# A decoder layer on one core: masks and context requested earlier, the convolution by four groups, and filters without the D_skip products

## Time and profile before

| | us |
|---|---|
| median of 3 runs | 7834.85 (7827.19 to 7838.27) |
| profiled execution, time | 7831.92 |
| its span | 7830.1 |
| setup, to its end | 194.0 |
| pass 1 | 5297.0 |
| pass 2 | 202.0 |
| pass 3 | 2137.1 |

### The profile page before, as it was taken

One profiled execution on the slowest core, in us unless ns is written; L12 is line 12 of the kernel. 1 busy time (PEld: TensorE's weight loads), 2 busy tenths in 40 slices (PEclk: granted clock), 3 DMA queues, 4 the chain that ended last, 5 costly groups with the idle time before them and its releaser, 6 DMA issues. The chain is left out here.

```text
span 7830.1 us, 109010 instructions
## 1 busy us (share of the span) xinstructions
PE 6972.0 (89%) x25744; PEld 3853.7 (49%) x25744; DVE 5404.5 (69%) x13954; ACT 4454.2 (57%) x9788; POOL 4638.6 (59%) x3991
## 2 busy tenths in 40 slices
PE   4799999999999999999999999996569999999997
PEld 2344444444444444444444444443535655556554
DVE  4477888778887888778877788776235555555554
ACT  1677887778777877777877887774211111111111
POOL 0588888888888888888888888884011111111111
PEclk5899999999999999999999999997889999999998
DMA  0465555555565555655555555552720000000000
GB/s 18 108 148 139 141 133 139 152 136 137 130 149 143 141 134 136 152 138 138 131 149 143 141 134 136 154 135 69 239 75 33 33 30 30 30 30 30 30 30 19
DMA packets 489840, 843.53 MB, mean 108 GB/s; under 512 B 35612, under 2 KB 139174, under 8 KB 487594
## 3 DMA queue, kind: packets, MB, share of 16 engines
q1 hardware_dynamic: 472234, 820.42, 41.2%
q10 hardware_dynamic: 17024, 16.78, 0.6%
HBM read 754.24 MB, written 82.84 MB: 107 GB/s over the span
## 5 line engine op out<-in xcount | busy, mean ns | idle before, releaser
L1203 POOL TENSOR_TENSOR arena<-arena 128x512 f32<-128x512 f32 x2048 | 2593.3, 1282 | 286.9 <-DVE arena L1128 245.6
L825 PE MATMUL psum<-arena 128*128 128x512 f32 x4096 | 2216.5, 636 | 216.5 <-POOL arena L1203 209.4
L1128 DVE TENSOR_TENSOR_SCAN arena<-arena,psum 128x512 f32<-128x512 f32 x1024 | 1238.0, 1209 | 386.3 <-ACT arena L997 294.7
L1216 POOL TENSOR_TENSOR arena<-arena 128x512 f32<-128x512 f32 x1024 | 1347.5, 1316 | 113.4 <-PE psum L825 113.3
L984 ACT ACTIVATE arena<-arena 128x128 f32<-128x128 f32 x4096 | 1303.1, 395 | 129.9 <-PE psum L810 129.7
L1132 DVE TENSOR_TENSOR_SCAN arena<-psum,arena 128x512 f32<-128x512 f32 x1024 | 1237.5, 1208 | 107.1 <-ACT psum L997 41.4
L825 PEld LDWEIGHTS psum<-arena 128*128 128x128 f32 x4096 | 714.4, 201 | 775.0 <-POOL arena L1203 422.0
L1800 POOL TENSOR_SCALAR arena<-arena 128x4 f32<-128x4 f32 x160 | 36.8, 230 | 1262.4 <-DVE arena L1666 1262.3
L997 ACT ACTIVATE arena<-arena 128x508 f32<-128x508 f32 x1024 | 737.6, 720 | 58.4 <-DVE arena L1128 57.6
L810 PEld LDWEIGHTS psum<-arena 128*128 128x128 f32 x4096 | 525.4, 147 | 489.8 <-issue 446.6
L997 ACT ACTIVATE psum<-arena 128x508 f32<-128x508 f32 x1024 | 699.7, 683 | 65.2 <-DVE arena L1132 31.7
(11 more groups left out here) (216 smaller groups left out, 10588.2 us busy)
## 6 DMA issues: line engine op xcount, KB each, us to landing
arena<-bc_scratch SPq DMA_DIRECT2D x1152, 512.0 KB, 5.1
arena<-in_xT_dram SPq DMA_DIRECT2D x32, 512.0 KB
arena<-in_x_dram SPq DMA_DIRECT2D x32, 512.0 KB, 8.6
x_scratch<-arena SPq DMA_DIRECT2D x32, 512.0 KB, 5.8
xin_scratch<-arena SPq DMA_DIRECT2D x64, 256.0 KB, 3.1
arena<-kernel_scratch SPq DMA_DIRECT2D x32, 512.0 KB, 4.0
arena<-y_scratch SPq DMA_DIRECT2D x32, 512.0 KB
arena<-x_scratch SPq DMA_DIRECT2D x32, 512.0 KB, 3.7
```

What stands on the lines that cost most here:

```text
L825: pe.matmul(y_ps, ident, ring[:, u % RING], start=False, stop=n == NS - 1).then_inc(S["nsum"], 1)
L1128: dve.tensor_tensor_scan(s, decay_sb[:, u // 2 % 2], bx_ps[:, u // 2 % 2], 0.0, ALU.mult, ALU.add)\
L1203: pool.tensor_tensor(h, h, Cb[:, u // 2 % PAIRS, u % 2], ALU.mult).then_inc(S["hc"], 1)
L1216: pool.tensor_tensor(ring[:, u % RING], uu[par][:, c], Bb[:, state(u)], ALU.mult)\
```

## The change

- In pass 1 the masks and the transposed context are no longer requested at v = 2 of the block that uses them, but at v = 16 of the block before (`load_ahead`), once the block before that has used them. What stays in `load_back` is x and the context.
- `xin_scratch` and `y_scratch` have four groups of 64 channels. Pass 1 stores a block with four transfers in rows of 256 B instead of two in rows of 512 B; pass 3 loads y with four transfers in rows of 256 B instead of one in rows of 4 KB.
- Pass 2 runs by these groups. ACT issues all loads of x, and two of the first four tables; SP issues the other tables and all stores. A group is stored when its two rounds are read out. The loops are written out, and a bank of PSUM is waited for alone instead of with its whole round. Rows of x and y are now 16 KB in both directions.
- In setup the second product of each channel goes. `D_skip` is added by eight DVE operations of 8 x 32 elements after ACT's copies, from a tile whose last row it is loaded into.

```diff
             for q in range(8):
                 for dd in range(32):
-                    pe.matmul(o, tab[:, NR:NR + NG, d], tab[:, 0:NR, d], start=True, stop=False)
-                    mm = pe.matmul(o, last8, drow[:, d], start=False, stop=True)
+                    mm = pe.matmul(o, tab[:, NR:NR + NG, d], tab[:, 0:NR, d], start=True, stop=True)
                 mm.then_inc(kmm, 1)
...
+            for q in range(8):
+                dve.wait_ge(ksb, q + 1)
+                own = at_last[:, 32 * q:32 * q + 32]
+                dve.tensor_tensor(own, own, dsk[:, 32 * q:32 * q + 32], ALU.add).then_inc(skipped, 1)
...
-                need(sp, "k_mm", i - 1, 1)
+                need(sp, "xa_mm", i - 1, 2)
+                sp.dma_start(ctxn, i_["ctx"][:, bass.ts(i, G), :]).then_inc(S["ld_ctx"], 16)
+
+            def load_ahead(i):
+                need_apart(sp, ("maskb", i - 1, 1), ("tmb", i - 1, 1), ("k_mm", i - 1, 1))
+                sp.dma_start(tmask8, ...); sp.dma_start(mask8, ...)
                 sp.dma_start(ctxT0, ...); sp.dma_start(ctxT1, ...)
...
-                for h in range(DH):
-                    sp.dma_start(xin_d[h][:, bass.ts(i, G), :], xn[:, :, h * P:(h + 1) * P]).then_inc(S["st_xin"], 16)
+                for g in range(D // DG):
+                    sp.dma_start(xin_d[g][:, bass.ts(i, G), :], xn[:, :, g * DG:(g + 1) * DG])\
+                      .then_inc(S["st_xin"], 16)
...
+                    if v == 16:
+                        load_ahead(i)
...
+            load_toeplitz(sp, 0, 0)
+            load_toeplitz(sp, 0, 1)
+            for q in range(1, ROUNDS):
                 for k in range(NB_):
+                    sp.wait_ge(turned[k], q)
+                    load_toeplitz(sp, q, k)
+                if q > PER_GROUP and q % PER_GROUP == 1:
+                    store_y(q // PER_GROUP - 1)
+            store_y(D // DG - 1)
...
-                            pe.wait_ge(out_s if n % 2 else out_v, q * NB_)
+                            pe.wait_ge(out_s if n % 2 else out_v, (q - 1) * NB_ + n // 2 + 1)
...
+            load_toeplitz(act, 0, 2)
+            load_x(act, 0)
+            load_toeplitz(act, 0, 3)
+            for g in range(1, D // DG):
+                load_x(act, g)
...
-                    sp.dma_start(y, y_d[:, bass.ts(i, G), :]).then_inc(S["g_y"], 16)
+                    for g in range(D // DG):
+                        sp.dma_start(y[:, :, g * DG:(g + 1) * DG], y_d[g][:, bass.ts(i, G), :]).then_inc(S["g_y"], 16)
```

More of the change, by code:

```diff
@@ L29 @@
 DH = D // P
+DG = 64
 DI = 512
@@ L1246, in pass2 @@
     NB_ = 4
-    LOOPS = P // (GD * NB_)
+    ROUND = GD * NB_
+    ROUNDS = D // ROUND
+    PER_GROUP = DG // ROUND
     with ExitStack() as ctx:
@@ L1250, in sem @@
             return sems.named(n)
-        x_ld = [sem(f"x_ld{h}") for h in range(DH)]
+        x_ld = [sem(f"x_ld{g}") for g in range(D // DG)]
         t_ld = [sem(f"toeplitz_ld{k}") for k in range(NB_)]
@@ L1255, in pass2 @@
         cv = Carve(arena)
-        x2 = [cv.f32(B * P).rearrange("p (b d) -> p b d", b=B) for _ in range(DH)]
+        x2 = [cv.f32(B * DG).rearrange("p (b d) -> p b d", b=B) for _ in range(D // DG)]
         rev, tz = ([cv.f32(GD * L).rearrange("p (d j) -> p d j", d=GD) for _ in range(NB_)] for _ in range(2))
         block = ctx.enter_context(nc.Block())
[L1259 to L1270, removed]
+        def load_x(eng, g):
+            for q in range(2):
+                w = B // 2
+                eng.dma_start(x2[g][:, q * w:(q + 1) * w], xin_d[g][:, q * w:(q + 1) * w]).then_inc(x_ld[g], 16)
+        def load_toeplitz(eng, q, k):
+            row = kr_d[q * ROUND + k * GD:q * ROUND + (k + 1) * GD, :]
+            src = bass.AP(row.tensor, row.offset, [[1, P], [2 * L, GD], [1, L]])
+            eng.dma_start(rev[k], src).then_inc(t_ld[k], 16)
@@ L1272, in _, with channels @@
+        def channels(q, first, n):
+            d = q % PER_GROUP * ROUND + first
+            return x2[q // PER_GROUP][:, :, d:d + n]
         @block.sync
         def _(sp):
-            def load_toeplitz(q, first):
-                for k in range(NB_):
[L1277 to L1293, removed]
+            def store_y(g):
+                w = B // 2
+                for h in range(2):
+                    sp.wait_ge(out_v, NB_ * PER_GROUP * (g + 1))
+                    sp.wait_ge(out_s, NB_ * PER_GROUP * (g + 1))
+                    sp.dma_start(y_d[g][:, h * w:(h + 1) * w], x2[g][:, h * w:(h + 1) * w]).then_inc(y_st, 16)
@@ L1296, in _ @@
+            load_toeplitz(sp, 0, 0)
+            load_toeplitz(sp, 0, 1)
+            for q in range(1, ROUNDS):
+                for k in range(NB_):
+                    sp.wait_ge(turned[k], q)
[3 more added lines that the diff above has]
+            store_y(D // DG - 1)
+            sp.wait_ge(y_st, 16 * 2 * (D // DG))
         @block.tensor
         def _(pe):
-            def products(h, q, first):
+            for q in range(ROUNDS):
+                if q % PER_GROUP == 0:
+                    pe.wait_ge(x_ld[q // PER_GROUP], 16 * 2)
@@ L1302, in products @@
                         n = 2 * k + j
-                        if not first:
-                            pe.wait_ge(out_s if n % 2 else out_v, q * NB_)
+                        if q:
+                            pe.wait_ge(out_s if n % 2 else out_v, (q - 1) * NB_ + n // 2 + 1)
                         for dd in range(4):
-                            d = k * GD + j * 4 + dd
-                            col = x2[h][:, :, bass.ds(q * (NB_ * GD) + (d - h * P), 1)]
+                            col = channels(q, 4 * n + dd, 1)
                             pe.matmul(psum[:, n, dd * B:(dd + 1) * B], tz[k][:, j * 4 + dd],
@@ L1311, in products, with turn @@
                               .then_inc(conv_mm, 1)
[L1313 to L1328, removed]
-            copy(tz[k], rev[k][:, :, ::-1]).then_inc(turned[k], 1)
+        def turn(eng, copy, k, q):
+            eng.wait_ge(t_ld[k], 16 * (q + 1))
+            if q:
+                eng.wait_ge(conv_mm, (q - 1) * ROUND + (k + 1) * GD)
+            copy(tz[k], rev[k][:, :, ::-1]).then_inc(turned[k], 1)
@@ new lines, in read_out @@
+        def read_out(eng, odd, sem_, copy, turns):
+            for k in turns:
+                turn(eng, copy, k, 0)
+            for q in range(ROUNDS):
+                for n in range(odd, 2 * NB_, 2):
+                    eng.wait_ge(conv_mm, q * ROUND + 4 * (n + 1))
+                    copy(channels(q, 4 * n, 4).rearrange("p b d -> p d b"),
+                         psum[:, n, 0:4 * B].rearrange("p (d b) -> p d b", d=4)).then_inc(sem_, 1)
+                    if q + 1 < ROUNDS and n // 2 in turns:
+                        turn(eng, copy, n // 2, q + 1)
@@ L1331, in _ @@
         @block.gpsimd
         def _(pool):
[L1333 to L1340, removed]
-                    eng.wait_ge(conv_mm, q * (NB_ * GD) + 4 * (n + 1))
-                    dst = x2[h][:, :, bass.ds(q * (NB_ * GD) + (4 * n - h * P), 4)]
-                    copy(dst.rearrange("p b d -> p d b"),
-                         psum[:, n, 0:4 * B].rearrange("p (d b) -> p d b", d=4)).then_inc(sem_, 1)
-                    if ahead and n // 2 in turns:
-                        turn(eng, copy, n // 2, q + 1, False)
-            for k in turns:
-                turn(eng, copy, k, 0, True)
-            for h in range(DH):
-                last = h == DH - 1
-                with eng.Fori(h * LOOPS, (h + 1) * LOOPS - last, 1) as q:
-                    one_round(h, q, True)
-                if last:
-                    one_round(h, DH * LOOPS - 1, False)
+            for q in range(ROUNDS):
+                turn(pool, pool.tensor_copy, 0, q)
@@ L1362, in _ @@
         def _(act):
[L1363 to L1364 removed]
+            load_toeplitz(act, 0, 2)
[3 more added lines that the diff above has]
+                load_x(act, g)
             read_out(act, 1, out_s, act.copy, (2,))
[L1366 to L1369 removed]
 PER3 = dict(
[L1374 removed]
+    g_y=64, g_x1=16, g_xa=32, st_out=16,
     fo_mm=4, fo_mul=4, fo_add=4, xt=1, hn0=4, hn1=4, ht_mm=2, hT=2,
```

49 lines of the change are left out of this document (18 added, 31 removed).

## The result

The changed kernel takes 7473.8 us (median of 4 runs, 7461.07 to 7475.96) against 7831.02 (4 runs) before: a ratio of 0.954 [0.9523, 0.9556], or 357 us less. The prediction said 307 us less, 7525, with a range of 7455 to 7645. The profiled execution took 7475.96 us; its span is 7474.2.

| us | before | after | measured | predicted |
|---|---|---|---|---|
| setup | 194.0 | 133.6 | -60.4 | -39 |
| pass 1 | 5297.0 | 5039.9 | -257.1 | -237 + 1.8 |
| pass 2 | 202.0 | 163.1 | -38.9 | -35 |
| pass 3 | 2137.1 | 2137.6 | +0.5 | +2.3 |

A forecast was written before the change was run, and what follows sets the result against it. POOL's wait for the mask transfer, with PE stalled behind it, was taken to hold pass 1. From 7831.92 us: -237 (pass 1) -39 (setup) -35 (pass 2) +1.8 +2.3 = -307, so 7525 us, range 7455 to 7645.

The forecast's parts named there:

- What bounds the kernel: Pass 1: POOL's 237.2 us idle before the mask step, 7.41 us each, makes PE wait 6.1 us per block.
- The two signs at the block's start: Pass 1: the third chunk's taps start near 8 us after the first's; PE's granted clock is 1.00 at block start.
- I take the wait itself, 7.41 us: Pass 1: removing POOL's mask wait returns its 7.41 us in each of 32 blocks, 237 us.
- The control (block 0): Pass 1's block without a mask step: taps' spacing 7.94 us against 13.96, so 6.02 of 6.61 us come back.
- PE's whole account comes back: Rival, pass 1: PE regains 6.1 us standing and 3.3 low clock per block; 300 instead of 237, 7462 us; chance 0.15.
- The first rival: Pass 1: another wait steps in, POOL waiting for the scans; half the gain, 7644 us, period above 155; chance 0.15.
- v = 16 costs nothing: Pass 1: SP's four extra transfers and a wait at v = 16 hardly delay the next C load; cost nothing.
- 256-byte rows: zero in the blocks: Pass 1: the x store's 2048 packets take 3.6 us instead of 1.8, hidden by the second C load's slack; cost zero.
- the terms +1.8 and +2.3: Packet-count costs of 256-byte rows: +1.8 us for the last store ahead of pass 2, +2.3 at pass 3's start.
- both products take an equal part: Setup: each filter's two products share 78.4 us equally, so dropping one saves 39.2; gain 39 us, low end 20.
- its own steps: Pass 2: PE starts 14.7 us in, stands 18 us for starved round 1 tables, then a shorter store tail; gain 35.
- The rival without starving: Pass 2: round 1's tables aren't starved beside the x loads; gain 55 instead of 35 us, 7505 us; chance 0.08.

The follow-up runs named there:

- masks ahead: The kernel before with only the masks and the transposed context requested at v = 16: 7573.95 us, ratio 0.9679.
- the step later: The kernel before with POOL's mask step at unit 12 instead of unit 4, every transfer left in place: 7582.4 us, ratio 0.9691.
- masks alone ahead: The changed kernel with the transposed context requested at v = 2 again and only the two masks at v = 16: 7476.37 us, ratio 0.9553.
- the two reordered kernels: The changed kernel with x groups 1 to 3 requested at rounds 0, 2, 4: 7460.26 us; with all pass 2 transfers on SP's queue: 7465.75 us.
- the second stall removed in this kernel: The changed kernel with PE's scores of the third sequence at unit 38 instead of 36, removing the wait at L779: 7476.96 us, ratio 0.9553.
- the pairs over 128 rows: The kernel before with each filter's second product summed over 128 rows, zeros but for the first, instead of one: 7778.27 us in one run.
- 24 smaller ones: The changed kernel with each x group loaded by eight transfers in rows of 4 KB instead of two of 16 KB: 7471.64 us, ratio 0.9544.

## Why the prediction was right, and where a size was off

- **What bounds the kernel: right.** POOL's wait for the mask, with PE behind it, was the largest thing to remove. Three kernels show it: masks ahead (pass 1 5042.1), the step later (5047.0), masks alone ahead (5038.6), against 5297.0. The two signs at the block's start came as named: spacing of the taps 7.69 us (near 8), clock 1.00.
- **Size of pass 1: 257 instead of 237.** The step "I take the wait itself, 7.41 us" was some 0.6 us per block too small. It counted POOL's wait and nothing for the clock. Measured, PE gives back 175.9 / 32 = 5.5 us of standing and 81.2 / 32 = 2.5 us of slow clock, 8.0 together; the two parts of PE's account had been 6.1 and 3.3. The period fell by 8.1 us, to 151.9 and not 152.6. The 20 us are less than the 29 by which the same pass differs between kernels (5025.7 to 5054.9). The averages of four kernels with the old pass 1 and four with the new one, 5293.4 and 5039.5, differ by 254, so the term was too small, by about 17. The control (block 0) had been read for POOL's and DVE's work only, and is one block that itself starts at low clock. The rival "PE's whole account comes back" (300) was farther off: 43 us too much, against 20 too little.
- **No other wait stepped in** at the block's start. The first rival would have had a period above 155.
- **v = 16 costs nothing: right**, within what can be seen. The mask line has no idle time, and POOL's largest wait before L1210 is for DVE's scans, not for C. That context and burst have no share was left open by the prediction and is shown by the kernel with the masks alone.
- **256-byte rows: zero in the blocks was right, and for the reason given (cover). The packet count behind the terms +1.8 and +2.3 was a poor measure.** Where the cover is missing the finer store costs 0.58 us per block, and that is SP's time for two more requests. The last store, alone ahead of pass 2, shows the same: from its first request to the first of pass 2 it is 5.73 us, and 5.18 before, so 0.55 more, where equal time per packet gave 1.8. Pass 3 took 2136.7 to 2137.1 us in the six kernels here with the old rows and 2137.0 to 2141.2 in the eight with the new ones. The averages differ by 1.6 us, against the 2.3; the single cases touch. The Trainium skill (DMA: Bandwidth & Descriptors, Specifications) has line rate lost below 512 B. No run here shows that for these stores.
- **Setup: the mis-sized term, 39 forecast and 60.4 measured.** The failed step is "both products take an equal part". Equal records do not mean equal parts: the second product's own work is 11 us (60.4 - 49.5), and 49.5 us was what alternating between the two shapes cost both. The record durations could not show it (194 and 186 ns beside a pace of 76.6, since records overlap). DVE's addition cost the 0.2 us expected.
- **Pass 2: 38.9 against 35, right by its own steps.** Start 17.1 us in (forecast 14.7), stalls 19.2 (18), end of PE 149.6 (149), tail 13.5 (17). Starving packet for packet stood as read: 143 and 142 packets in 5 us. The rival without starving was wrong for this order and about half right as an aim: of the 19 us the two reordered kernels recover 9.5 and 7.5.
- **The sum.** The 49 us between the forecast change of the span (-307) and the measured one (-356) are 21 from setup, 22 from pass 1 (the wait's size and the 1.8), 4 from pass 2 and 2 from pass 3, all on one side.

Open: what now sets the period of 151.9 us. PE is busy 94% of pass 1 and still gained nothing from a faster clock. That the loop of decay, scan and multiplication (ACT, DVE, POOL) holds it is likely from POOL's grown wait for the scans, and was not tested.

## What to carry to other kernels

An in-order engine pays for a transfer's latency at the first step that awaits it. Moving the request forward and moving the step back gave nearly the same here (252 and 243 us), so look for the cheaper of the two. Cutting a transfer into more requests costs the issuing engine's time for each, and what stands behind them in its list is asked for later. A stall of the bounding engine is worth its standing time and its slow clock after it only while nothing else is due at that place; the second stall removed in this kernel was worth nothing. Look at the pace of records (span over count), not at their durations, when many small instructions overlap.

## What the hardware did that was not expected

- Two requests more for the same 512 KB cost SP 1.4 us, and twice as many packets of half the size cost nothing that shows.
- Alternating matmuls of 128 rows and of 1 row ran at 74 to 77 ns per record, uniform ones at 28 to 34 ns, at a granted clock of 0.50 in both. The alternating stretches stayed at 0.50, though the profile shows PE without a gap in them; the uniform ones were at 1.00 from 107 us on. Why the pairs over 128 rows ran at 28.8 ns per record (1024 in 29.5 us) and the single products of the changed kernel at 34 is not settled.
- An engine can stand in its own requests, and its computation waits behind them: ACT took 1.14 us for its first two requests of x in the changed kernel and 14.35 us for the six others, and 35.84 us for 24 smaller ones. That its queue was full then is an inference.
- While both queues had work, they shared the DMA engines packet for packet, whatever the size: 143 to 142 with 16 KB against 512 B, 1291 to 1294 with rows of 4 KB.
